# Sample 0 pinned to the front of the order and fetched before the sort; coefficients computed sample-major and sorted by matmul; tables loaded from the ScalarE queue

## What is computed

```
x = x + x @ W0[subject].T + b0[subject]
a = amplitudes ** delta_t;  ang = frequencies * delta_t          # 64 pairs of tokens
x = x + rotate(x, a * cos(ang), a * sin(ang))                    # mixes tokens 2f and 2f+1
x = x + x @ W2[category] + b2[category]
h = relu(x @ W1[language] + b1[language])
y = x + h @ Wup[language] + bup[language]
x = x + layernorm(y) * gamma[language] + beta[language]
```

## Time and profile before

| what | value |
|---|---|
| median of 3 runs | 1203.55 us (1201.64 to 1204.3) |
| profiled execution, its time | 1206.43 us |
| profiled execution, its span | 1204.6 us |
| PE busy | 1133.4 us, 94% |
| DVE busy | 1025.5 us, 85% |
| POOL busy | 865.6 us, 72% |
| ACT busy | 583.4 us, 48% |
| first matmul of sample 0 | 27.59 us after the start |
| DMA over the span | 291.70 MB, mean 242 GB/s |

### The profile page before, as it was taken

How to read it: one execution, slowest core, us unless ns; L and a number is a source line. 1 busy time by engine, 2 the same in 40 slices (tenths; PEclk the granted TensorE clock), 3 DMA queues, 4 the chain that set the end, 5 groups by cost and what they waited for, 6 DMA issues and landing times.

```text
span 1204.6 us, 27886 instructions
## 1 busy us (share of the span) xinstructions
PE 1133.4 (94%) x5902; PEld 913.2 (76%) x5902; DVE 1025.5 (85%) x1465; ACT 583.4 (48%) x923; POOL 865.6 (72%) x792
## 2 busy tenths in 40 slices
PE   1899999999989999999998999989999999999996
PEld 1678878878768887877886788778787887777874
DVE  3398888998888898898888888988888888898887
ACT  2345455455455555445454545445445544544542
POOL 3966667886676677668767666876766677768884
PEclk9899999999999999999999899999998999999999
DMA  6967776777787687767767786787678678867772
GB/s 241 426 225 233 254 258 211 238 253 221 224 291 238 208 261 263 252 213 239 251 215 274 231 259 208 232 286 239 211 249 280 208 237 247 275 214 247 243 252 79
DMA packets 96407, 291.70 MB, mean 242 GB/s; under 512 B 11584, under 2 KB 11712, under 8 KB 78272
## 3 DMA queue, kind: packets, MB, share of 16 engines
q1 hardware_dynamic: 96192, 289.52, 73.3%
HBM read 255.93 MB, written 33.55 MB: 240 GB/s over the span
## 4 chain that ended last, share of the span: by engine, by line
SPq 37%; PE 34%; issue 18%; DVE 5%; DMA 2%; POOL 2%; DVEq 1%; ACT 1%; POOLq 0%; ACTq 0%
SPq L193 6%; SPq L199 5%; SPq L205 5%; PE ps_l L789 4%; PE ps_l L757 4%; PE ps_l L740 4%; PE ps_l L779 4%; PE ps_y L818 3%; PE ps_l L783 3%; PE ps_hT L809 3%; PE ps_mix L768 3%; SPq L196 3%; SPq L208 3%; SPq L202 3%; SPq L286 3%
## 5 line engine op out<-in xcount | busy, mean ns | idle before, releaser
L629 DVE TENSOR_TENSOR w_lo<-w_in,w_hi 128x1024 fp32r<-128x1024 f32 x256 | 330.2, 1330 | 0.0
L381 POOL TENSOR_TENSOR x_lo<-x_in,x_hi 128x512 fp32r<-128x512 f32 x128 | 166.0, 1297 | 160.4 <-DVE w_lo L629 157.1
L486 ACT ACTIVATE w_hi<-w_in 128x1024 fp32r<-128x1024 f32 x256 | 255.3, 1045 | 12.4 <-PE ps_l L783 12.4
L375 POOL TENSOR_TENSOR w_in<-w_in,ident 128x512 f32<-128x512 f32 x128 | 164.3, 1284 | 65.2 <-DMA w_in<-W 64.8
L451 ACT ACTIVATE ps_diag<-ident,cos 128x128 f32<-128x128 f32 x128 | 47.6, 372 | 304.9 <-DVE mix L604 304.6
L405 POOL TENSOR_TENSOR x<-x,beta_sb 128x512 f32<-128x512 f32 x128 | 174.3, 1361 | 28.9 <-POOL x3b L398 28.9
L768 PEld LDWEIGHTS ps_mix<-mix,x 128*128 128x128 f32 x1024 | 132.7, 191 | 73.4 <-issue 69.5
L398 POOL TENSOR_TENSOR x3b<-x,bup_sb 128x512 f32<-128x512 f32 x128 | 169.0, 1320 | 9.6 <-DVE x L651 9.6
L740 PE MATMUL ps_l<-w_hi,x_hi 128*128 128x512 f32 x512 | 154.8, 425 | 15.4 <-ACT w_hi L462 14.1
L789 PE MATMUL ps_l<-w_lo,x2T_hi 128*128 128x512 f32 x512 | 147.7, 401 | 11.6 <-DVE w_lo L629 11.4
L809 PE MATMUL ps_hT<-x3T,w_in 128*128 128x128 f32 x1024 | 138.7, 279 | 13.8 <-ACT x3T L507 13.8
(11 more groups left out here) (82 smaller groups left out, 1713.6 us busy)
## 6 DMA issues: line engine op xcount, KB each, us to landing
w_in<-W SPq DMA_DIRECT2D x128, 1024.0 KB, 6.3
b_in<-b SPq DMA_DIRECT2D x136, 256.0 KB, 5.8
x_in<-xT SPq DMA_DIRECT2D x128, 256.0 KB, 4.8
w_in<-W SPq DMA_DIRECT2D x128, 256.0 KB, 2.7
out<-yb SPq DMA_DIRECT2D x128, 256.0 KB, 5.4
w_in<-W0T SPq DMA_DIRECT2D x8, 1024.0 KB, 4.9
bup_sb<-bup SPq DMA_DIRECT2D x1, 2560.0 KB, 8.8
wup_sb<-Wup SPq DMA_DIRECT2D x1, 2560.0 KB, 10.6
```

The lines of the kernel that those rows point to most:

```text
L486: act.activation(w2_hi[:, halves[n]], w2_in[s % WB][:, halves[n]], ACT.Copy).then_inc(w2_hi_made, 1)
L629: dve.tensor_tensor(w2_lo[:, half], w2_in[s % WB][:, half], w2_hi[:, half].bitcast(fp32), ALU.subtract).then_inc(w2_lo_made, 1)
```

## The change

- Sample 0 comes first in the order: DVE subtracts 1024 from the key of every sample that has sample 0's subject (four more small operations). The subject groups then have 15 (subject 2), 15, 20, 20, 15, 14, 14 and 15 samples: the second change of weight comes at step 30 in place of 35.
- Sample 0's x, W0, b0, W2, b2 and W1 are fetched without waiting for the sort, with indices read from the freshly loaded rows.
- Angles, sines, cosines and powers are made with samples on partitions and the 64 frequencies along the row. The powers are two POOL pieces of 32 columns. DVE multiplies and duplicates them into 128 columns, PE sorts them with the one-hot matrix (`sort_coefficients`, between `l0_front(0)` and `l0_back(0)`), ACT and DVE copy them out. All 128 samples are done there; the later pieces are gone.
- delta_t, amplitudes, frequencies, one index column, b1 and the four tables are issued by ACT on its own queue; bup and Wup after W0 has landed, beta and gamma after W0 has been rounded.
- POOL adds beta for sample s-1 after `add_up_bias(s)`, in place of beta for sample s.

```
         @block.sync
-            sp.dma_start(irows[:, B:2 * B], subject.partition_broadcast(P)).then_inc(small_loaded, 16)
-            for n, ids_dram in enumerate((subject, category, language)):
-                sp.dma_start(icols[:, n + 1:n + 2], ids_dram.rearrange("a b -> b a")).then_inc(small_loaded, 16)
+            sp.dma_start(irows[:, B:2 * B], subject.partition_broadcast(P)).then_inc(subjects_loaded, 16)
+            for n, ids_dram in ((2, category), (3, language)):
+                sp.dma_start(icols[:, n:n + 1], ids_dram.rearrange("a b -> b a")).then_inc(small_loaded, 16)
...
-            load_x(0, 0, 0)
-            fetch_w0(subject_of(sp, 0))
+            sp.dma_start(x_in[0][:, :], xT[0:1].rearrange("o p c n -> p (o c n)")).then_inc(x_loaded[0], 16)
+            sp.wait_ge(subjects_loaded, 16)
+            fetch_w0(sp.value_load(irows[0:1, B:B + 1], min_val=0, max_val=S - 1))
+            sp.wait_ge(small_loaded, 16 * 6)
             load_w2(0, 0, 0)
             load_b2(0, 0, 0)
+            load_w1(0, 0, 0)
+            sp.wait_ge(ids_made, 2)
             load_x(1, 1, 1)
             load_w2(1, 1, 1)
...
         @block.gpsimd
+            pool.wait_ge(small_loaded, 16 * 6)
+            powers(slice(0, F // 2))
             rest_of_x(0)
             fold_w0(0)
+            powers(slice(F // 2, F))
             fold_w2(0)
+            pool.wait_ge(ids_made, 2)
             rest_of_x(1)
             fold_w2(1)
             fold_w0(1)
             fold_w0(2)
-            pool.tensor_tensor(power[:, LATER:], amp_col.broadcast_to([N, B - LATER]), dt_sb[:, LATER:], ALU.pow)\
-                .then_inc(power_made, 1)
             pool.wait_ge(bup_loaded, 16)
...
                 add_up_bias(s, lang)
-                add_beta(s, lang)
+                if s >= 1:
+                    add_beta(s - 1, lang_before)
...
         @block.scalar
             round_x(0)
+            act.wait_ge(w0_loaded, 32)
+            act.dma_start(bup_sb[:, :], table(bup)).then_inc(bup_loaded, 16)
+            act.dma_start(wup_sb[:, :], Wup.rearrange("p l d -> p (l d)")).then_inc(wup_loaded, 16)
             round_w0(0)
+            act.dma_start(beta_sb[:, :], table(beta)).then_inc(beta_loaded, 16)
+            act.dma_start(gamma_sb[:, :], table(gamma)).then_inc(gamma_loaded, 16)
+            act.wait_ge(angles_reduced, 1)
+            act.activation(sine, angle_sin, ACT.Sin).then_inc(trig_made, 1)
+            act.wait_ge(angles_reduced, 2)
+            act.activation(cosine, angle_cos, ACT.Sin).then_inc(trig_made, 1)
+            act.wait_ge(coef_sorted, 1)
+            act.activation(sin1[:, :], ps_mix[:, 0:B], ACT.Copy).then_inc(coef_made, 1)
...
         @block.vector
+            split_w0(0, 1)
+            coefficients()
+            split_w0(1, 1)
+            dve.wait_ge(coef_sorted, 1)
+            dve.tensor_scalar(cos1[:, :], ps_hT[:, :], 1.0, None, ALU.add).then_inc(coef_made, 1)
...
         @block.tensor
             l0_front(0)
+            sort_coefficients()
             l0_back(0)
+            pe.wait_ge(coef_made, 2)
             rotate(0)
+            pe.wait_ge(ids_made, 2)
```

More of the change, by code:

```diff
@@ L116, in conditioned_residual_stack @@
         cols = stats_cols[:, 0:5]
-        dt_col, amp_col, freq_col = (stats_cols[:, n:n + 1] for n in (5, 6, 7))
+        dt_col = stats_cols[:, 5:6]
         key_col, rank, earlier = (stats_cols[:, n:n + 1] for n in (12, 13, 14))
@@ L124, in conditioned_residual_stack @@
         same = x3T[:, 2 * B:3 * B]
-        dt_wide = x3T[:, 3 * B:4 * B]
         onehot = hT[:, :]
         reached = mix[:, :]
-        ang, turns, angle_sin, angle_cos = (x1[:, n * B:(n + 1) * B] for n in range(4))
-        dt_sb, power, sine, cosine = (x3[X3B - 1][:, n * B:(n + 1) * B] for n in range(4))
+        F = N // 2
+        amp_row, freq_row, sin_of, cos_of = (x3[1][:, n * N:(n + 1) * N] for n in range(4))
+        ang, turns, angle_sin, angle_cos = (x1[:, n * F:(n + 1) * F] for n in range(4))
+        power, sine, cosine = (x3[2][:, n * F:(n + 1) * F] for n in range(3))
+        subjects_loaded = sem("subjects_loaded")
         small_loaded = sem("small_loaded")
@@ L350, in _, with powers @@
                                base=-1, pattern=[[-2, N // 2]], channel_multiplier=1).then_inc(consts_made, 1)
[L352 to L355, removed]
             pool.wait_ge(consts_made, 3)
+            def powers(places):
+                n = places.stop - places.start
+                pool.tensor_tensor(power[:, places], amp_row[:, 2 * places.start:2 * places.stop:2],
+                                   dt_col.broadcast_to([P, n]), ALU.pow).then_inc(power_made, 1)
             def fold_w0(s):
@@ L586, in _, with coefficients @@
                 dve.tensor_scalar(red, red, PI_BELOW, -PI_BELOW, ALU.min, ALU.max).then_inc(angles_reduced, 1)
[L588 to L596, removed]
-            dve.wait_ge(consts_made, 3)
+            dve.wait_ge(sorted_done, 1)
+            dve.tensor_copy(ids[:, 0:4 * B], ps_x3T[0:1, :]).then_inc(ids_made, 1)
+            dve.tensor_copy(ids[:, 4 * B:6 * B], ps_l2[0:1, 0:2 * B]).then_inc(ids_made, 1)
+            dve.wait_ge(consts_made, 3)
+            def coefficients():
+                dve.wait_ge(power_made, 2)
+                dve.wait_ge(trig_made, 2)
+                for wide, trig in ((sin_of, sine), (cos_of, cosine)):
+                    dve.tensor_tensor(wide.rearrange("p (f e) -> p f e", e=2),
+                                      power.unsqueeze(2).broadcast_to([P, F, 2]),
+                                      trig.unsqueeze(2).broadcast_to([P, F, 2]), ALU.mult).then_inc(coef_wide, 1)
             def make_mix(s):
@@ L702, in _ @@
                     finish_l0(s + 1)
-                if s == X3B - 2:
-                    dve.wait_ge(power_made, 3)
-                    coefficients(slice(SOON, B))
-                    dve.wait_ge(coef_made, 4)
                 if s >= 1:
```

96 lines of the change are left out of this document (43 added, 53 removed).

## The result

The changed kernel takes 1191.95 us (median of 6 runs, 1191.32 to 1196.06) against 1203.08 for the kernel before (6 runs): ratio 0.9922, 95% interval 0.9904 to 0.9939. That is 11 us faster where 3.7 were forecast. The profiled execution took 1191.34, with a span of 1189.5; the profile of before lies 3.4 us above its median, so the two spans differ by 15.1 and not by 11.

What follows compares the result with a forecast made beforehand. PE, busy 94% of the span, was taken to bound the kernel away from the edges, DMA the start. Of 17.1 us in three terms DMA left 3.9, less 0.2 at the end: 1203.55 - 3.7 = 1199.8; range 1189 to 1204.5.

Steps and rivals of the forecast that it cites:

- the forecast side: Whole kernel: faster, given 0.66, against same 0.18 and slower 0.16.
- the mechanism of the start: Start of the kernel: bound by DMA, so most of the earlier start is taken back; 1198 to 1203, chance 0.5.
- Term 1: Prologue to sample 0's first product: fetch ahead brings `finish_l0(0)` at 23.5 against 32.98, 9.5 us.
- Terms 2 and 3: Early steps: 96-column power with PE's wait and slow clock goes, 6.2 us; late coefficients go, 1.4 us.
- term 2: Sample 2 to 3: the 96-column power, PE's wait and the slow clock behind it go, 6.2 us.
- What DMA takes back: Start up to `centre(0)`: 21.8 MB must land, so DMA limits the gain; 3.9 us left.
- the end with the tables first: Start, queues served packet by packet: tables in at 42, x(1) 34.4, x(2) 44; gain 1.7 to 4.8 us.
- the net of the start: Start, after DMA's share is taken back: 3.9 us faster.
- The moved change of weight: Second change of weight, step 35 to 30: bounded by +4.5 and -1 us, taken as nothing.
- Nothing for the steps: Steps away from the start: keep 8.55 us each, `add_beta` a step later costs nothing.
- room on the DMA: Rival for the start: DMA has room, all terms hold, 15 to 17 us faster, 1186.7; chance 0.13.
- the share in between: Rival for the start: tables get about 70% of the bytes, 6 to 11 us faster, 1195; chance 0.18.

Runs made afterwards that it cites:

- e8: Changed kernel with the four table loads put back on SP's queue: 1187.79 us, ratio 0.9866 to the kernel before.
- e2: Kernel before with only the new sample order, sample 0's subject first: 1200.92 us, ratio 0.9995 to the kernel before.
- e7: Changed kernel with SP's repeated loop of 12 steps written out for all steps: 1174.75 us, ratio 0.9762 to the kernel before.
- e10: Kernel before with SP's loop written out for all steps: 1174.78 us, ratio 0.9804 to the kernel before.
- e1: Kernel before with only the beta addition moved a step later: 1201.84 us, ratio 1.0004 to the kernel before.
- e3: Changed kernel with the beta addition back in its old place: 1190.45 us, ratio 0.9920 to the kernel before.
- e5: Changed kernel with 13 idle semaphore instructions on SP ahead of its loop: 1204.57 us, ratio 0.9994 to the kernel before.
- e6: Kernel before with 13 idle semaphore instructions on SP ahead of its loop: 1191.44 us, ratio 0.9893 to the kernel before.
- e9: Changed kernel with each table loaded as two transfers, even and odd languages, in 2 KB rows: 1194.83 us, ratio 0.9981 to the kernel before.

## Why the prediction was right and why wrong

The time lay in the range and on the forecast side, and the mechanism of the start was the forecast one, but that it was faster at all was luck: the start, the only part from which the forecast took a gain, lost 1.0 us, and all of the gain came from the steps, for which it took nothing.

- *Term 1, 9.5 us for the fetch ahead:* measured 6.9. The small loads were in at 7.5 and not at 5.2: the last was the column of subjects, issued by ACT at 2.14, fourth on its queue, which took 5.3 us. POOL's first powers ran from 7.62, the fold at 14.31, the first matmul at 17.70 (15.7 forecast). From the end of `l0_front(0)` at 19.80 to `l0_back(0)` at 23.48 it was 3.7 us, 2.8 of them PE's wait for the coefficients (2.2 forecast in all).
- *Terms 2 and 3:* the power of 96 columns and the late coefficients went; step 4 took 8.55. The 6.2 of term 2 did not show, as a longer stall took the place of the old one.
- *What DMA takes back:* right in kind, and the end with the tables first was the true one: x(1) landed at 31.1 (34.4 forecast), x(2) at 48.5 (44), gamma at 47.2, before x(2). The Trainium skill's page "DMA: Bandwidth & Descriptors", section "Queues, rings and completion order", has the DMA engines go round the queues a packet at a time; the trace agrees, with 211 packets of SP's queue to 215 of ACT's from 31 to 43 us. The step that was mis-sized is the net of the start: 3.9 forecast, -1.0 measured. The bytes moved at 371 to 406 GB/s from 10 to 25 us and not at 423. And PE was granted 0.50 of its clock, 1.2 of 2.4 GHz, from 20 to 25, from 30 to 35 and from 50 to 55 us, where the sum had it once; in e8 it had 1.00 in every stretch from 10 to 55.
- *The moved change of weight, +4.5 to -1, taken as nothing:* 4.9 in the profile of the changed kernel, 4.4 in e2's, of which the runs of e2 show nothing; with SP's loop written out it is gone (e7, e10).
- *Nothing for the steps:* the step that failed, and with it its premise that away from the edges the time is PE's. It had nothing to do with `add_beta`, to which the prediction tied it (e1, e3). SP has no time in hand in its loop, and what counted was a thing that the prediction did not cost at all, the length of SP's program ahead of that loop: about 11 us in the profiles (10 at steps 35 to 127).
- *The rivals:* room on the DMA was refuted by the GB/s (412 to 431 from 25 to 50 us), and the share in between by the packets and by x(2), at 48.5 and not at 36.5. Yet the measured 1191.95 is nearer to the times of these two, 1186.7 and 1195, than to the forecast 1199.8. A time that fits is no evidence for a mechanism.

How the profile could have shown it: in before the waits of 3 and 1.4 us behind L324, at nine repeats, stand in SP's chain. They were passed over as the cost of a loop that the change didn't touch. The Trainium skill's page "Advanced Engine Details and Errata", section "ISA Cache", says that a sequencer keeps two lines of 256 instructions. A pass of the loop runs 576 or 584, so by that page a jump back finds its target gone. The trace agrees as far as it goes: it has the fetch behind each jump, and 3 us as its price; a loop short enough to stay was not run. The second wait is for the next piece, whose edge lies at number 280. Here the trace has pieces of 8 KB and stops every 112 instructions, where it doesn't count those that a branch skips, not every 256.

## What to carry to other kernels

Look at what SP does at the repeats of its loop when transfers come late every so many samples, and at how long it waits for others: an issuing engine that hardly waits has no time in hand. A kernel with a rolled issue loop is to be compared with another only with that loop written out or in the same place, or a change is credited with what its length did. A second DMA queue is no free lane: rows of 20 KB on it starve rows of 2 KB on the other, and small rows can hold the engine that issues them. When a start is bound by bytes, an earlier first matmul is given back at the next load.

## What the hardware showed that I had not expected

- 13 instructions without effect, on no engine that computes, make one kernel 0.7% slower (0.9994 against 0.9922, e5) and another 1.1% faster (0.9893, e6).
- A transfer of 1.3 MB in rows of 2 KB, issued by ACT while others were in flight, held ACT's queue for 12.4 us (e9); twice the bytes in rows of 20 KB took it 0.33 to 0.51.
- Where POOL's additions run beside DVE's subtraction, the pair of subtractions takes 4.48 us in place of 2.35 and one addition 2.00 in place of 1.27.
- Two loaded queues move as many packets each, whatever the size of their rows: 211 to 215 with 1.09 and 4.06 MB.
